# One-hot rows of a graph network: column numbers and weights read from PSUM, one wide vector instruction cut into eight short ones in the layers

## What is computed

```
net 0, five layers:  h_in = h + vn
                     emsg = relu(h_in[src] + edge_attr @ We[l] + be[l])
                     agg  = segment_sum(emsg, dst);  t = MLP(h_in + agg);  h = bn(t) (+ relu) + h_in
net 1, weighted:     agg  = segment_sum(x[src] * edge_weight, dst);  agg @ W_rel + x @ W_root, batch norm
net 2, attention:    msg  = h[src] * coef (softmax over the edges of a target);  segment_sum(msg, dst)
net 3, three convs:  h = h @ W;  segment_sum(h[src] * dinv[src] * dinv[dst], dst);  relu between
```

## Time and profile before

| What | Value |
|---|---|
| three executions, median | 7895.26 us |
| profiled execution, own time | 7899.28 us |
| its span, first to last instruction | 7897.5 us |
| PE, DVE, ACT, POOL busy | 6096.5, 3614.1, 1615.2, 5301.3 us |
| gathers (line 375 and, in attention, 1368) | 4608 and 512 |
| one-hot instructions of line 267 and of line 919 | 705 and 310 |
| weight multiplications, line 564 | 128 |

### The profile page before, as it was taken

The page is one execution under the profiler, slowest core; times in us unless marked ns, Lnnn a source line. Parts: engine busy times, 40 slices in busy tenths (PEclk is TensorE's granted clock), DMA queues, the critical chain, the costliest instruction groups (busy, mean ns, idle before and its releaser), DMA issues. The chain is left out here.

```text
span 7897.5 us, 114763 instructions
## 1 busy us (share of the span) xinstructions
PE 6096.5 (77%) x28483; PEld 4573.2 (58%) x28484; DVE 3614.1 (46%) x5667; ACT 1615.2 (20%) x3223; POOL 5301.3 (67%) x5128
## 2 busy tenths in 40 slices
PE   4789778978977895797677746666778878887877
PEld 3678567756865784686456634454534554554445
DVE  5566445544644554566344545555622221232223
ACT  2333222222222222232000234333210000000000
POOL 4777577677757766775777265443067767777777
PEclk8899889989998998899788967777866886786688
DMA  5444444444444444444333176554233333333333
GB/s 134 130 135 131 124 129 131 123 130 132 132 122 131 131 127 122 133 140 124 96 95 93 55 254 216 198 184 157 86 97 103 104 97 100 104 103 89 101 106 100
DMA packets 434491, 986.80 MB, mean 125 GB/s; under 512 B 124176, under 2 KB 210832, under 8 KB 417936
## 3 DMA queue, kind: packets, MB, share of 16 engines
q0 software_dynamic: 245760, 673.51, 29.6%
q1 hardware_dynamic: 128816, 194.88, 7.5%
q10 hardware_dynamic: 59744, 116.68, 4.3%
HBM read 845.23 MB, written 139.46 MB: 125 GB/s over the span
## 5 line engine op out<-in xcount | busy, mean ns | idle before, releaser
L375 POOL DMA_INDIRECT ring<-node_table,idx x4608 | 4772.2, 1036 | 1922.4 <-issue 1864.3
L386 PE MATMUL psE<-ring,shared 128*128 128x256 f32 x3072 | 1226.8, 528 | 391.2 <-DMA ring<-node_table,idx 227.4
L991 DVE TENSOR_TENSOR ring<-ring,psE 128x1024 f32<-128x1024 f32 x640 | 777.2, 1220 | 1212.4 <-DMA ring<-node_table,idx 1078.4
L386 PEld LDWEIGHTS psE<-ring,shared 128*128 128x128 f32 x3072 | 653.6, 244 | 929.8 <-DMA ring<-node_table,idx 610.2
L1368 POOL DMA_INDIRECT ring<-att_table,idx x512 | 528.2, 1032 | 609.8 <-ACT idx L1572 333.7
L855 ACT ACTIVATE ring<-ring 128x1024 f32<-128x1024 f32 x640 | 663.7, 1060 | 1238.4 <-DVE ring L991 1237.2
L695 PE MATMUL psE<-we_stk,stk 128*128 128x256 bf16 x2560 | 407.0, 296 | 490.4 <-DVE ring L991 460.4
L267 DVE SCALAR_TENSOR_TENSOR shared<-iota,block_start,dst_f 128x1024 f32<-128x1024 f32 x352 | 449.9, 1284 | 627.5 <-PE psE L386 526.7
L386 PE MATMUL psAT<-ring,S 128*128 128x256 f32 x2560 | 676.0, 424 | 0.0
L386 PE MATMUL psAT<-ring,shared 128*128 128x256 f32 x2560 | 672.3, 423 | 0.0
L386 PEld LDWEIGHTS psAT<-ring,S 128*128 128x128 f32 x2560 | 544.0, 218 | 94.5 <-issue 4.9
(11 more groups left out here) (356 smaller groups left out, 7051.1 us busy)
## 6 DMA issues: line engine op xcount, KB each, us to landing
ring<-node_table,idx POOLq DMA_INDIRECT x4608, 2.8
rows_table<-ring SPq DMA_DIRECT2D x64, 1072.0 KB, 4.1
ring<-rows_table ACTq DMA_DIRECT2D x64, 1072.0 KB, 5.4
stk<-stack_table SPq DMA_DIRECT2D x128, 512.0 KB, 3.9
node_table<-tab ACTq DMA_DIRECT2D x251, 128.0 KB
stack_table<-stk SPq DMA_DIRECT2D x64, 256.0 KB, 2.2
ring<-att_table,idx POOLq DMA_INDIRECT x512, 3.0
tab<-in_x ACTq DMA_DIRECT2D x35, 128.0 KB
```

Source lines behind the costliest of these rows:

```text
L375: nc.gpsimd.indirect_dma_start(ring[:, q, 0:gw], None, table, bass.IndirectOffsetOnAxis(ap=idx[:, RING * half + q:RING * half + q + 1], ax ...
L386: ins = nc.tensor.matmul(bank, hots[:, u, :], ring[:, U * ob + u, 0:D], start=False, stop=True, skip_group_check=True)
L991: nc.vector.tensor_tensor(ring[:, q:q + 4, 0:D], ring[:, q:q + 4, 0:D], psE[:, 4 * D * g:4 * D * g + 4 * D].rearrange("p (u f) -> p u f", ...
```

## The change

Three things are changed.

- In the weighted pass and in each convolution, DVE first copies the column numbers from `iota` into the third bank of `psE` (`columns`), in the weighted pass also the 512 weights a partition into the fourth (`weight_ps`). `hot_unit` then reads the column numbers from there, and line 564 the weights.
- In the layers `hot_unit` is replaced by `hot_tiles`: eight `tensor_scalar` instructions, one for each tile, on 128 elements. The input is `iota` in SBUF; block start and target number are both scalars for each partition.
- The further one-hot matrix of the layers, up to now two instructions of 512 elements, is made by `hot_tiles` too.

```diff
+        columns = psE[:, 1024:1024 + P]
+
         def hot_unit(out, h, blk):
 
             return nc.vector.scalar_tensor_tensor(
-                out, iota[:, :].unsqueeze(1).to_broadcast([P, U, P]), block_start[:, bass.ds(blk, 1)],
+                out, columns.unsqueeze(1).to_broadcast([P, U, P]), block_start[:, bass.ds(blk, 1)],
                 dst_f[:, bass.ds(U * h, U)].unsqueeze(2).to_broadcast([P, U, P]), ALU.add, ALU.is_equal)
+
+        def hot_tiles(outs, h, blk):
+
+            for u, out in enumerate(outs):
+                ins = nc.vector.tensor_scalar(out, iota[:, :], block_start[:, bass.ds(blk, 1)],
+                                              dst_f[:, bass.ds(U * h + u, 1)], ALU.add, ALU.is_equal)
+            return ins
...
+            weight_ps = psE[:, 1536:1536 + NT]
...
                     nc.vector.memset(AGG[:, :], 0.0)
+                    nc.vector.tensor_copy(columns, iota[:, :])
+                    nc.vector.tensor_copy(weight_ps, weight[:, :])
...
                                     ring[:, q:q + 4, 0:D], ring[:, q:q + 4, 0:D],
-                                    weight[:, bass.ds(RING * i + q, 4)].unsqueeze(2).to_broadcast([P, 4, D]),
+                                    weight_ps[:, bass.ds(RING * i + q, 4)].unsqueeze(2).to_broadcast([P, 4, D]),
...
                     def further_hots(h, b):
-                        for g in range(2):
-                            ins = nc.vector.scalar_tensor_tensor(
-                                hot_halves[g], iota[:, :].unsqueeze(1).to_broadcast([P, 4, P]),
-                                block_start[:, bass.ds(b, 1)],
-                                dst_f[:, bass.ds(U * h + 4 * g, 4)].unsqueeze(2).to_broadcast([P, 4, P]),
-                                ALU.add, ALU.is_equal)
+                        ins = hot_tiles([hot_halves[u // 4][:, u % 4, :] for u in range(U)], h, b)
                         ins.then_inc(hot_further, 1)
...
-                            hot_unit(hot_sets[(ob + 1) % 2], octet_behind(h), then).then_inc(hot_first, 1)
+                            hot_tiles([hot_sets[(ob + 1) % 2][:, u, :] for u in range(U)], octet_behind(h), then).then_inc(hot_first, 1)
...
                     dve.reg_mov(at_dve, (NO + 1) * (n + 1) + 1)
+                    nc.vector.tensor_copy(columns, iota[:, :])
```

More of the change, by code:

```diff
@@ L977, in _ @@
                     if l == 0:
-                        hot_unit(hot_sets[0], 0, 0).then_inc(hot_first, 1)
+                        hot_tiles([hot_sets[0][:, u, :] for u in range(U)], 0, 0).then_inc(hot_first, 1)
                     with dve.Fori(0, NG) as i:
```

## The result

The changed kernel takes 7564.1 us (median of four, 7562.29 to 7569.23), the kernel before in the same comparison 7889.56 us (four, 7878.99 to 7897.6). The ratio is 0.9589, with a 95% interval of 0.9573 to 0.9606: 325 us less. Forecast were 286 us less and 7610 us; the range began at 7570, 6 us above what came. The direction, the mechanism of the stalls and the order of the parts were right. The sum was too small: the term of the last layer rested on a wrong bound (2 us forecast, 14 measured), part 1 gave 19 us more than forecast, and 12 us came from a pass whose code is the same in both.

A forecast was written before the change was run, and what follows sets the result against it. The prediction took POOL's chain of gathers to bound the kernel. From the 7895.3 us median it took 202 us (weighted pass, convolutions) and 84 us (layers), giving 7609, rounded to 7610 us; range 7570 to 7745 us.

The forecast's parts named there:

- the mechanism of the stalls: All walks: certain DVE instructions hold something a gather needs, so it waits; 399 us in all.
- the term of the last layer: Last layer: gathers save 30 us, but longer DVE trains set the pace, so only 2 us stay.
- part 1: Weighted pass and convolutions: column numbers and weights from PSUM remove the stalls; -202 us.
- The moment at 0.13 us: Every gather: some 0.13 us after its start it needs something that certain DVE instructions hold.
- the first and third property: DVE holds: an instruction with one PSUM input doesn't hold; a hold begins with the data, not the instruction.
- The reserve of 7 us for PE's queue: Weighted pass and convolutions: 3 and 4 us taken off the gain for a small PE queue at the end.
- rival C: Weighted pass and convolutions: PE can't follow, a third of 202 us is lost; 7677 us, chance 0.09.
- Part 2: Layers' stalls: short instructions leave 5 us a layer; gathers save 26 us (layers 1 to 3), 46 (layer 0), 30 (last).
- Part 3: Layers: longer DVE trains add 2.15 us to an octet with a second one-hot; -84 us remain for the layers.
- its wait for POOL: Layers' trains: DVE must wait for POOL in 1.7 stretches of 0.12 us each, 0.2 us a train.
- Layers 1 to 3: In these layers PE sets the pace late; some 20 of 26 us a layer arrive, 60 us in all.
- layer 0: This layer has the longest queue; half of the 46 us its gathers save arrives, say 22 us.

The follow-up runs named there:

- e5: Changed kernel, but the layers' eight short one-hot instructions are scalar_tensor_tensor with two SBUF inputs; 7626.9 us, ratio 0.9666.
- e6: Changed kernel, but the last layer makes its one-hots as before, wide from SBUF; 7585.69 us, ratio 0.9612.
- e8: Kernel before with 17 more short DVE instructions ahead of the weighted pass; 7882.05 us, attention 1195.0 us (one execution).
- e9: Changed kernel with 24 more short DVE instructions ahead of the weighted pass; 7573.56 us, attention 1203.2 us (one execution).

## Why the prediction was right and where it was wrong

**The stalled gathers: right.** The moment at 0.13 us, the 0.82 us behind the end of the hold, and the first and third property carried over to the changed kernel (for the third, e5 has a form where a hold doesn't always end between neighbours). A wide comparison with its column numbers in PSUM stalls nothing, in any phase. POOL, then DVE, first convolution of the changed kernel:

```profile
5589.11 0.94 POOL L384 DMA_INDIRECT ring<-node_table,idx  x1 [0.30 <-issue]
```

```profile
5588.27 1.28 DVE L269 SCALAR_TENSOR_TENSOR S<-psE,block_start,dst_f 128x1024 f32<-128x1024 f32 x1 [3.07 <-PE psE L395]
```

The moment, 5589.24, lies 0.97 us into the comparison, which goes on to 5589.55; the gather takes 0.94 us. In the weighted pass and the convolutions 348 gathers have their moment deep inside such an instruction; the shortest takes 942, the longest 958 ns. In the earlier trace rows the same pair cost 0.72 us.

**Part 1, -202: too small by 19.** What stays was set at 1.5 us in each of the four walks and 8.0 for the bias; against 485.9 us the walks stand at -1.1, -1.0, -0.8 and 6.8 us (other small instructions stall 0.3 to 1.0 us a walk, and the mean gather is a few ns below 0.949; the bias is 8.2): 10 us of the 19. The reserve of 7 us for PE's queue wasn't needed: PE follows, so rival C falls (PE's busy time in the second convolution even fell from 580.6 to 558.6 us, the clock rising from 0.74 to 0.77 of full speed). Each was small and each on the safe side, and caution in the same direction every time is a bias. (The first sum of the prediction, 399 us of stalls with layers 2 and 3 at 30 each, comes to 400; nothing hangs on it.)

**Part 2, what short instructions stall: right in size.** Forecast 5 us a layer; 5.5, 5.0, 4.9 and 5.4 came, and 13.8 in layer 0, whose casts for the edge features stall on. The working behind it was off: in layers 1 to 4 a train meets 1.5 moments and not 1.7, and 236 of 577 are caught (41%), not a quarter, for 0.05 us each and not 0.03. The hold lasts 0.11 us (moments 0.13 to 0.02 us before the end) and not 0.07. That is 0.03 us a train, twice the 0.015 of the forecast, 2.8 us a layer in place of 1.4; the round 5 us a layer that was left for trains and other instructions covered it, which is luck of the reserve and not of the working. The Trainium skill (SBUF — State Buffer, Who interferes with whom) has the shared ports locked for the whole of a DVE instruction in a two-port mode; if the short instructions run in one, that would catch all 577, and the measurement decides against it in this case: whether a gather is caught depends on where in the instruction its moment falls.

**Part 3, the length of a train: nearly right; its wait for POOL: wrong.** Forecast 346 ns and one start every 0.26 us, in all 2.2 us. The last layer, DVE, then POOL:

```profile
3465.09 2.13 DVE L276 TENSOR_SCALAR shared<-iota,block_start,dst_f 128x128 f32<-128x128 f32 x8
3467.14 0.41 DVE L937 TENSOR_TENSOR tin<-psV,bias_row 128x256 f32<-128x256 f32 x1
```

```profile
3465.30 0.95 POOL L384 DMA_INDIRECT ring<-node_table,idx  x1 [0.30 <-issue]
3466.55 0.98 POOL L384 DMA_INDIRECT ring<-node_table,idx  x1 [0.30 <-issue]
```

2.13 us, with two gathers beside it. Single instructions do wait for POOL: of the 3,808 in trains 681 take over 0.36 us (0.45 on the mean, the others 0.34, which is why the mean is 359 ns), and 622 of the 681 end 0.04 to 0.06 us after a gather does. But the next one starts on time, 0.26 us after the start of the long one, so the train isn't longer: 2.15 us is the mean of all 476. The 0.2 us a train were nothing.

**The last layer, -2 forecast and -14 measured: the step that failed.** The prediction set DVE's own cycle at 10.7 us, the length of one octet, added 2.15 and so had DVE set the pace. But that octet was the shortest of four. The four cycles from its start are 10.7, 11.4, 11.5 and 12.4 us, the mean 11.5, and over them PE was busy throughout. Before, then after, four octets with a second one-hot each:

```profile
3590.29:3636.35 46.06, 46.06 (x266) 41.37 (x266) 33.18 (x60) 15.04 (x33) 35.99 (x34) 1.00 0.47 140
```

```profile
3462.82:3510.92 48.10, 46.77 (x264) 40.19 (x263) 39.32 (x112) 14.64 (x33) 36.53 (x38) 1.00 0.50 147
```

PE 46.06 of 46.06 us, DVE 33.18: the bound was PE, as in layers 1 to 3, and DVE had room. After the change DVE is busy 39.32 of 48.10 us, 1.5 us an octet more, PE is idle for 1.3 us, and the cycle has grown by 0.5 to 12.0, not by 2.2 to 12.9. Two starts show one cycle of the four, 11.80 us:

```profile
3462.82 2.35 DVE L999 TENSOR_TENSOR ring<-ring,psE 128x1024 f32<-128x1024 f32 x2 [0.56 <-issue]
3474.62 2.35 DVE L999 TENSOR_TENSOR ring<-ring,psE 128x1024 f32<-128x1024 f32 x2 [0.54 <-issue]
```

The kind of loss was right: gathers run ahead, and the way from the last gather of this layer to the first of the weighted pass grew from 46.7 to 62.5 us (forecast 25 more, 16 came). So of the 30 us that the gathers save 14 arrive. e6 shows both sides of it.

**Layers 1 to 3: right; layer 0: right by luck.** Layers 1 to 3 gave -62.9 for -60, with the way from the last gather to the first of the next walk 48.6, 47.1 and 49.7 us instead of 43.7, 43.9 and 45.3, 3 to 5 longer where 5 to 8 were forecast. Layer 0 gave -24.0 for -22, but its gathers saved 37 us and not 46 (13.8 stay), and the queue took 13 of them and not 24: two errors that cancel. Six waits for a full ring stand there, 15 us together, where the kernel before had one of 3 us.

**Attention, 0 forecast and -12: not in the argument at all.** e8 and e9 show that it comes from the place of the code. Without it the kernel would take about 7576 us, inside the range. Attention, the last layer and the three convolutions missed by 12 us each, the weighted pass by 7 and layers 0 to 3 by 5: 48 us by which the sum fell short. The lower end of the range, 7570, was set by the layers alone, at a gain of 123 us; they gained 101. What went below it is the 19 us of part 1 and the 12 us of attention, for which the range left nothing.

**The median.** The gain against the medians is 39 us larger than forecast while the time is 46 us lower: the kernel before ran 6 us lower beside the changed one than in the runs that the forecast started from.

## What to carry to other kernels

When GpSimd issues the DMAs that set the pace, look for gathers that are longer than their median and at which DVE instruction they end; here moving one input of that instruction to PSUM removed the stall at no cost on DVE, and where PSUM was full, short `tensor_scalar` instructions with a single SBUF input removed most of it (35 of 177 us stayed in the layers), while short ones with two left 116 us. Take an engine's cycle as the mean over the pattern's whole period and read in the same window which engine has no idle time left, before adding a cost to it. After a change that adds or removes instructions, compare a stretch whose code is the same: if it moved, that part of the gain belongs to the place of the code, and a few padding instructions tell it apart.

## What the runs showed of the hardware that was not expected

- A stalled gather can miss the end of a hold and wait for the end of the next, up to the fifth: 89 of 431 in e5, and 0 of 236 where the short instructions have one SBUF input.
- The hold of a 128-element instruction with one SBUF input begins about 0.21 us after its start (0.34 less the 0.13 of the earliest moment that is stalled), with two about 0.18 us (0.344 less 0.165).
- DVE pauses at fixed places of its program (0.34 us ahead of line 1855, in every fourth octet). With the same instructions in the attention pass, the place of the code made 1195 or 1208 us of it, 0.16% of the kernel, nearly what two kernels must differ by to be told apart; the located pauses are 5 of these 13 us.
- Of DVE instructions in a train the one that waits for POOL is 0.11 us longer on the mean (681 of 3,808), and the train is not.
